# Splitting the next head's first weight piece at another place of the step

## The reference

```python
q = jnp.einsum('bsd,ed->bse', x, Wq).reshape(bsz, seqlen, HQ, D)
k = jnp.einsum('bsd,ed->bse', x, Wk).reshape(bsz, seqlen, HK, D)
v = jnp.einsum('bsd,ed->bse', x, Wv).reshape(bsz, seqlen, HK, D)
q = _rope(_rmsnorm(q, q_norm_w), pos)
k = _rope(_rmsnorm(k, k_norm_w), pos)
k_all = jnp.concatenate([k_cache[block_table]..., k], axis=1)   # 512 cached keys and 128 new ones
v_all = jnp.concatenate([v_cache[block_table]..., v], axis=1)
scores = jnp.einsum('bqhd,bkhd->bhqk', q, k_all) * SCALE
probs = jax.nn.softmax(jnp.where(valid, scores, -1e+30), axis=-1)
o = jnp.einsum('bhqk,bkhd->bqhd', probs, v_all)
return jnp.einsum('bse,de->bsd', o, Wo)
```

## Time and profile before

| | us |
|---|---|
| median of 3 runs | 1377.78 |
| lowest and highest run | 1377.43, 1379.28 |
| the profiled execution, its own time | 1378.39 |
| its span, first to last instruction | 1376.6 |

### The profile page before, as it was taken

One profiled execution on the slowest core, in us unless ns is written; L12 is line 12 of the kernel. 1 busy time (PEld: TensorE's weight loads), 2 busy tenths in 40 slices (PEclk: granted clock), 3 DMA queues, 4 the chain that ended last, 5 costly groups with the idle time before them and its releaser, 6 DMA issues.

```text
span 1376.6 us, 23429 instructions
## 1 busy us (share of the span) xinstructions
PE 1358.4 (99%) x8007; PEld 1182.4 (86%) x8007; DVE 1226.7 (89%) x2623; ACT 870.7 (63%) x2224; POOL 783.0 (57%) x813
## 2 busy tenths in 40 slices
PE   8899999999999999999999999999999999999998
PEld 6788888888888888888888888888888887888887
DVE  8999898989898989898989898999899987977783
ACT  7777676767676767676767676767777662222221
POOL 6867666666676667666766666666666610111111
PEclk9999999999999999999999999999999999999999
DMA  6111111111111111111111111112121321111112
GB/s 209 52 47 46 55 55 47 47 55 55 47 46 55 55 46 47 54 54 47 47 55 54 47 46 55 55 47 79 40 73 32 114 96 45 47 47 62 62 47 70
DMA packets 33889, 80.44 MB, mean 58 GB/s; under 512 B 10242, under 2 KB 11266, under 8 KB 32354
## 3 DMA queue, kind: packets, MB, share of 16 engines
q1 hardware_dynamic: 17378, 45.29, 10.6%
q0 software_dynamic: 16384, 33.59, 8.4%
HBM read 76.74 MB, written 2.10 MB: 57 GB/s over the span
## 4 chain that ended last, share of the span: by engine, by line
PE 86%; DVE 8%; ACT 3%; issue 1%; DMA 1%; POOL 0%; SPq 0%; DVEq 0%; ACTq 0%
PE proj_ps L111 10%; PE proj_ps L113 10%; PE proj_ps L112 10%; PE turn_ps L768 9%; PE score_ps L113 5%; PE score_ps L112 5%; PE score_ps L111 5%; PE value_ps L111 5%; PE value_ps L112 5%; PE value_ps L113 5%; PE gu_ps L111 2%; PE gu_ps L113 2%; PE gu_ps L112 2%; PE turn_ps L730 2%; PE turn_ps L737 2%; PE out_ps L1035 1%
## 5 line engine op out<-in xcount | busy, mean ns | idle before, releaser
L559 POOL DMA_INDIRECT kg<-kc,idx x256 | 263.6, 1030 | 264.3 <-issue 248.6
L1286 ACT ACTIVATE probs<-probs,shift,rstd 128x640 f32<-128x640 f32 x256 | 234.5, 918 | 132.7 <-DVE shift L1730 132.7
L569 POOL DMA_INDIRECT vg<-vc,idx x256 | 253.3, 989 | 70.7 <-issue 70.6
L1766 DVE TENSOR_TENSOR pt_lo<-turn_ps,pt_hi 128x512 fp32r<-128x512 f32 x320 | 217.6, 685 | 41.6 <-ACT pt_hi L1292 39.9
L1292 ACT ACTIVATE pt_hi<-turn_ps 128x512 fp32r<-128x512 f32 x320 | 186.5, 593 | 86.6 <-PE turn_ps L768 86.2
L1741 DVE CUSTOM_DVE_ANT_0 probs<-score_ps,mask 128x640 f32<-128x640 f32 x256 | 206.5, 821 | 10.5 <-PE score_ps L113 8.5
L768 PE MATMUL turn_ps<-cst,probs 128*128 128x128 f32 x1280 | 191.6, 272 | 1.6 <-DVE probs L1759 0.9
L111 PE MATMUL proj_ps<-w_hi,xt_parts 128*128 128x512 f32 x496 | 188.9, 381 | 0.7 <-ACT qk L1242 0.7
L768 PEld LDWEIGHTS turn_ps<-cst,probs 128*128 128x128 f32 x1280 | 157.2, 141 | 28.2 <-DVE probs L1759 2.2
L113 PE MATMUL proj_ps<-w_hi,xt_parts 128*128 128x512 f32 x496 | 168.1, 339 | 0.0
L112 PE MATMUL proj_ps<-w_lo,xt_parts 128*128 128x512 f32 x496 | 167.1, 337 | 0.0
(11 more groups left out here) (255 smaller groups left out, 3310.7 us busy)
## 6 DMA issues: line engine op xcount, KB each, us to landing
w_raw<-wqkv SPq DMA_DIRECT2D x28, 384.0 KB, 3.3
wo_raw<-wo SPq DMA_DIRECT2D x32, 256.0 KB, 3.1
wa_sb<-wa SPq DMA_DIRECT2D x7, 1024.0 KB, 4.9
kg<-kc,idx POOLq DMA_INDIRECT x256, 2.7
vg<-vc,idx POOLq DMA_INDIRECT x256
wg_raw<-wg SPq DMA_DIRECT2D x2, 1376.0 KB, 6.2
wu_raw<-wu SPq DMA_DIRECT2D x1, 2752.0 KB, 12.5
wd_raw<-wd SPq DMA_DIRECT2D x1, 2560.0 KB, 12.9
```

Source lines behind the costliest of these rows:

```text
L559: pool.indirect_dma_start(kg[:, b % 2, c, :], None, kc, bass.IndirectOffsetOnAxis(ap=idx[:, s // B % 2, b * NC + c:b * NC + c + 1], axis=0))\
L569: pool.indirect_dma_start(vg[:, b % 2, c, :], None, vc, bass.IndirectOffsetOnAxis(ap=idx[:, s // B % 2, b * NC + c:b * NC + c + 1], axis=0))\
L1286: act.activation(row, row, ACT.Exp, bias=shift[:, h:h + 1], scale=rstd[:, b % 2, h:h + 1], accum_out=sums[:, h:h + 1])\
L1766: dve.tensor_tensor(pt_lo[:, at, :], turn_ps[1 - j % 2][:, :], pt_hi[:, at, :].bitcast(F32), ALU.subtract).then_inc(p_lo_done[j], 1)
```

## The change

Two edits. On ScalarE, the rounding of piece 0 of the next group's weights moves from behind the copies of probabilities 3 and 4 to ahead of them, right behind the exponentials of heads 2 and 3. On VectorE, the subtraction for piece 0 moves from behind the low part of probabilities 4 to behind the low parts of the cached keys and the queries, ahead of that of the new key; and the scaling of heads 2 and 3 goes behind the low parts of probabilities 3 and 4 instead of ahead of them. No instruction is added or taken away, and no semaphore changes.

```diff
@@ ScalarE, step @@
                         if live(s + 1):
                             exps(s + 1, b1, (2, 3))
+                        if next_w:
+                            split_w(g + 1, 0)
                         ...
                         if live(s):
                             split_probs(s, b, 4)
                         ...
-                        if next_w:
-                            split_w(g + 1, 0)
                         if live(s + 3):
                             copy_q(s + 3)
@@ VectorE, step_with_first_w @@
                         split_probs(s, b, 2)
-                        normalise(s + 1, b1, (0, 1, 2))
+                        normalise(s + 1, b1, (0, 1))
                         split_probs(s, b, 3)
+                        normalise(s + 1, b1, (2,))
+                        split_probs(s, b, 4)
                         normalise(s + 1, b1, (3,))
-                        split_probs(s, b, 4)
-                        split_w(g + 1, 0)
                         split_cached_k(s + 2)
                         split_q(s + 2)
+                        split_w(g + 1, 0)
                         split_new_k(s + 2)
```

## The result

| | median us | lowest, highest | runs |
|---|---|---|---|
| before | 1377.87 | 1377.43, 1379.28 | 12 |
| after | 1380.63 | 1379.66, 1382.08 | 12 |

The ratio is 1.0019, 95% interval 1.0012 to 1.0026: the changed kernel is slower by 2.8 us. The prediction said slower by 6.0, and 1383.8. The direction holds and the time lies in the range, but the size is off by more than half.

What follows compares the result with a forecast made beforehand. TensorE, busy 99%, was taken as the bound, late by 0.37 us per place. Six places losing 0.9 and one 0.5 gave 5.9, taken as 6 us: median 1377.78 becoming 1383.8, range 1378.0 to 1386.5.

Steps and rivals of the forecast that it cites:

- ScalarE's part: Weights' rounding right behind the exponentials, from 528.94; copy of probabilities 3 starts at 529.89, 0.05 late; nothing lost.
- VectorE's chain: Low parts on VectorE: weights start at 534.49, new key at 535.64, 0.54 later than before, output at 537.12.
- The wait did move: TensorE's wait for the cached keys' low part goes, gaining 0.32; the scores wait for the new key's instead, repaying it.
- The meeting: VectorE's subtraction for weights piece 1 starts 0.20 behind GpSimd's for the values and is held, ending 1.10 later; chance 0.68.
- The next step: Step behind the hold: VectorE's lag of 0.97 at the maximum of head 2 reaches TensorE as 0.8 lost.
- What the hold costs: Prediction's section following the held VectorE through its queue to TensorE's next step: 0.9 to 1.0 us per place.
- the late projection: Output projection on TensorE starts at about 537.95 in place of 537.86: 0.1 us lost per place.
- If the row of the scaling is no longer held, 0.5 less: Alternative for the two scaled rows on VectorE, without their hold: 0.5 us less than the 0.9 to 1.0 per place.
- GpSimd's index instruction: Said to hold VectorE's scaling of two rows, which took 1.45 where two unheld rows take 0.93.
- the lower bound of one place: Loss per place of 0.4 us, if the scaling is not held and there is some unseen slack; upper bound 1.3.
- The chances: Overall: faster 0.03, within 0.32, slower 0.65; parts: hold 0.68, only moved wait 0.23, wait gone 0.07, unnamed slower 0.02.

Runs made afterwards that it cites:

- e3_no_meeting: Changed kernel, with GpSimd waiting for VectorE's subtraction of weights piece 1 before its own subtraction for the values; 1379.00 us, 1.0009 of the kernel before.
- e5_lag_once: Kernel before, plus one unread mask maximum on VectorE behind the low part of weights piece 1, seven times; 1380.03 us, ratio 0.9992.
- e6_lag_twice: Kernel before, plus two unread mask maxima on VectorE behind the low part of weights piece 1, seven times; 1380.13 us, ratio 0.9999.
- e4_more_lag: Changed kernel, plus one unread mask maximum on VectorE behind the subtraction for weights piece 1, seven times; 1382.99 us, 1.0039 of the kernel before.
- x1_index_moved: Kernel before, with GpSimd's index instruction moved from behind the four value gathers to between the second and third; 1377.37 us, ratio 0.9999.

## Why the prediction was half right

**ScalarE's part** held: the rounding started at 529.01 and the copy of probabilities 3 at 529.96, less the 0.08 between the two traces 528.93 and 529.88, against 528.94 and 529.89.

**VectorE's chain** held: weights at 534.48 (predicted 534.49), new key 535.61 (535.64), output 537.08 (537.12), each less 0.08. The wait did move from the cached keys to the scores. The output projection lost 0.05 where I had 0.10.

**The meeting** held: VectorE's lead was -0.16 for -0.20, the duration 2.21, GpSimd's back at 1.29. e3_no_meeting shows that the hold is a real part of the loss.

**The next step is where it failed.** The step is the one in *What the hold costs* by which VectorE's lag of 0.97 reaches TensorE as 0.8 (0.9 with the late projection); the runs show 0.37. The prediction took the scaled rows over with the 1.45 of the earlier trace rows, its words being that it "moves to 547.80, its end, and with it the low part of probabilities 3, from 548.16 to 549.2". In after, counted from the start of the place (531.24, 531.32):

| | before | predicted lag | measured lag |
|---|---|---|---|
| maximum of head 2 | 10.44 | 0.97 | 0.88 |
| reciprocals | 15.34 | 1.02 | 0.77 |
| probabilities' low part | 16.92 | 1.04 | 0.38 |
| weight load of the cached keys (predicted: TensorE's loss) | 17.65 | 0.9 | 0.37 |

Of the 0.66 by which the low part was less late than predicted, 0.39 are the rows (1.06 for 1.45) and 0.25 the lag of the reciprocals. Part of the latter is in the rows too: the `shift` of head 2 took 0.15, not the 0.23 it took before. The last line holds once the third is right: what the low part is late, TensorE is late. The slack of 0.1 to 0.15 that the prediction put between the two did not show.

The reason is that a held instruction is not a property of its place. With VectorE 0.8 later, its piece 2 no longer starts 0.89 ahead of the fourth gather (545.43, 546.32) but 0.23 ahead (546.30, 546.53). In both cases the gather ends 2.04 to 2.05 behind the start of piece 2, as if it began at 1.10, when piece 2 is nearly through.

What differs is how soon VectorE is at the first scaled row: 1.36 behind the start of piece 2 in before, 1.34 in after. Read in nanoseconds, over all kernels in which the gather starts during piece 2 and runs into the rows, the first row is free at all 45 places where it starts up to 1.351 behind piece 2, and held at all 18 where it starts from 1.353 on. At the held ones the gather started 0.88 to 0.99 behind piece 2; at 42 of the free ones it started 0.70 behind or less. A held row ends 2.35 to 2.36 behind piece 2, so 1.25 to 1.26 behind the 1.10 of the gather: the figure of the 41 rows. So two hundredths of a microsecond decide over 0.39, and a lag that moves piece 2 closer to the gather's start frees the rows. Why VectorE is those 0.02 later when the gather starts near the end of piece 2 stays open.

That a lag by itself frees the rows is shown by e5_lag_once and e6_lag_twice, which have nothing of the change. Some of the added lag is absorbed ahead of the rows and 0.39 by the rows; e4_more_lag shows that from there on the rest passes one to one.

The prediction had this case, "If the row of the scaling is no longer held, 0.5 less", and then took the other. It also named the wrong instruction as the holder, GpSimd's index instruction. And its 0.5 sets 1.45, from the first start to the last end, against 0.93, twice the 0.47 from one unheld row's start to the next one's; like for like the rows gave 0.39. Whether the hold would end could hardly be computed, since it hangs on 0.02. But that it stood at its edge could be seen. The trace of before had a pair of rows that were not held, at the second place:

```profile
271.00 1.06 DVE L1759 TENSOR_SCALAR probs<-probs,recips 128x640 f32<-128x640 f32 x2
```

At the other six they took 1.40 to 1.50. The free pair started 1.350 behind piece 2, the others 1.358 to 1.410.

The rest of the sum was sound: with 0.4 per place, the figure that stands as the lower bound of one place, seven places give 2.8. The chances are off by 0.01 in their own sum: the parts give 0.66 for slower and 0.31 for within.

## What to carry to other kernels

A wait that is removed on the busiest engine by putting work ahead of something else on another engine mostly moves; the chain to the next consumer says at once whether it is paid back. When an engine is delayed, each duration behind it that contains a hold must be worked out afresh, with the other engine's own new times: here a delay of 0.88 caused by one hold ended another, and only 0.37 reached TensorE. Before a drawn-out instruction is taken as given, compare it at all its repeats: one that is short at one of seven places is near its edge. And before a holder is named, look at the held instruction by itself: an instruction that starts only after the held one should have ended is not what held it.

## What the runs showed of the hardware

- A subtraction of VectorE with both inputs in SBUF took 2.21 instead of 1.22 us when it started 0.16 behind GpSimd's subtraction of 1.29 us, and ended about 1.1 behind it. With a lead of 0.58 to 0.61 it took 1.22, and GpSimd's was drawn out to 1.76 to 1.81. The page SBUF — State Buffer of the Trainium skill ("Who interferes with whom") has it that such a pair contends; these rows agree.
- A gather of GpSimd is drawn out by VectorE's subtraction as well: from 0.95 to 1.82 us when it started 0.23 inside one, to 1.34 from 0.69 inside, while the subtraction kept its 1.22. Wherever in the subtraction it started (0.20 to 0.99 behind), it ended 2.03 to 2.05 behind the subtraction's start.
- A gather draws out a scaled row of VectorE (128x640 float32, one input tile) that starts some way into it: 0.73 in place of 0.55 us at 0.53 behind the gather's start, 41 times, and 0.63 at 0.63 behind (x1_index_moved), each ending about 1.26 behind the start of the gather. A row that started 0.16 behind it took its 0.55.
- A single-column instruction can be held for much longer than it lasts: `shift`, 0.15 us when alone, took 0.85 beside GpSimd's subtraction in e3_no_meeting.
